# A decay recurrence as a scan on VectorE, or as a TensorE product with a triangular matrix of decay powers

## The reference

```python
DECAY = 0.95
scale = jnp.float32(np.sqrt(1.0 - DECAY))
gate = jax.nn.sigmoid(jnp.einsum('bse,em->bsm', x, Wg) + bg)
store = jnp.einsum('bse,em->bsm', x, Wv) * gate * scale
mem = smear(store, DECAY)      # mem[s] = DECAY * mem[s-1] + store[s], along the tokens
que = jax.nn.sigmoid(jnp.einsum('bse,em->bsm', x, Wq) + bq)
load = mem * que * scale
return jnp.einsum('bsm,me->bse', load, Wo)
```

```python
x = x + _L0_attn_ref(_layernorm(x, axis=-1), ...)
x = x + _L0_xattn_ref(_layernorm(x, axis=-1), ctx_512, ...)   # sim -> normalised over 256 keys -> softmax, added to x
x = x + _L0_ffn_ref(_layernorm(x, axis=-1), ...)              # argmax router, expert of each token, shared expert
```

## Time and profile before

| what | value |
| --- | --- |
| time, median of 3 executions | 166.57 us (164.66 to 167.26) |
| span of the profiled execution, first to last instruction | 155.8 us |
| TensorE busy | 119.9 us, 77% |
| VectorE busy | 108.1 us, 69% |
| GpSimd busy | 101.7 us, 65% |
| ScalarE busy | 69.8 us, 45% |

### The profile page before, as it was taken

One profiled execution on the slowest core, in us unless ns is written; L12 is line 12 of the kernel. 1 busy time (PEld: TensorE's weight loads), 2 busy tenths in 40 slices (PEclk: granted clock), 3 DMA queues, 4 the chain that ended last, 5 costly groups with the idle time before them and its releaser, 6 DMA issues. The chain is left out here.

```text
span 155.8 us, 2769 instructions
## 1 busy us (share of the span) xinstructions
PE 119.9 (77%) x709; PEld 97.2 (62%) x710; DVE 108.1 (69%) x303; ACT 69.8 (45%) x164; POOL 101.7 (65%) x145
## 2 busy tenths in 40 slices
PE   0199997997599658669879794459999979999700
PEld 0158986993387338347659594327878859888500
DVE  2672596949897999999699977122676866776510
ACT  3445878494396726794344401011434333343100
POOL 5346695696588828967858578605377776777540
PEclk9999999999999999975899999965999999999975
DMA  5997465236222251440222258283243334111000
GB/s 141 229 279 211 157 184 157 68 83 192 65 52 85 71 135 23 120 126 0 74 70 69 103 203 299 84 268 103 77 113 104 117 101 148 50 58 44 31 0 0
DMA packets 18206, 17.51 MB, mean 112 GB/s; under 512 B 4108, under 2 KB 17424, under 8 KB 18192
## 3 DMA queue, kind: packets, MB, share of 16 engines
q1 hardware_dynamic: 15792, 13.56, 30.8%
q0 software_dynamic: 1824, 3.22, 6.5%
q10 hardware_dynamic: 576, 0.56, 1.1%
HBM read 13.78 MB, written 5.38 MB: 123 GB/s over the span
## 5 line engine op out<-in xcount | busy, mean ns | idle before, releaser
L437 POOL TENSOR_TENSOR gu_lo<-stage,gu_hi 128x512 fp32r<-128x512 f32 x16 | 22.4, 1410 | 2.8 <-ACT gu_hi L502 2.8
L452 POOL DMA_INDIRECT tq<-base_rows,tid x15 | 15.4, 1026 | 13.1 <-DMA base_rows<-res 6.2
L457 POOL DMA_INDIRECT out_dram<-z,tid x15 | 15.2, 1012 | 7.6 <-DVE tid L851 2.6
L478 ACT ACTIVATE xn<-res,shift,rstd 128x256 f32<-128x256 f32 x22 | 12.0, 593 | 8.2 <-POOL shift L413 8.1
L405 POOL TENSOR_SCALAR vareps<-mv 128x2 f32<-128x2 f32 x16 | 4.2, 259 | 15.7 <-DVE mv L673 15.0
L409 POOL TENSOR_TENSOR rstd<-vareps,expo 128x2 f32<-128x2 f32 x16 | 12.4, 772 | 0.4
L1057 PE MATMUL bV<-shd,xn 128*128 128x256 f32 x32 | 9.6, 453 | 2.0 <-DVE xn L818 2.0
L670 DVE BATCH_NORM_STATS2 bn<-res 128x6 f32<-128x256 f32 x24 | 8.9, 413 | 3.0 <-DMA res<-in_x_dram 3.0
L437 POOL TENSOR_TENSOR dn_lo<-stage,dn_hi 128x512 fp32r<-128x512 f32 x8 | 11.0, 1371 | 0.0
L432 POOL DMA_INDIRECT x_sorted<-xs,dest x8 | 8.2, 1031 | 4.0 <-issue 2.6
L982 PE MATMUL bO<-wo,tq 128*128 128x256 f32 x32 | 7.8, 386 | 3.8 <-issue 2.8
(11 more groups left out here) (200 smaller groups left out, 386.4 us busy)
## 6 DMA issues: line engine op xcount, KB each, us to landing
stage<-in_L_ffn_gate_w_dram SPq DMA_DIRECT2D x8, 256.0 KB, 2.8
...
```

The costliest lines, as they stand in the source:

```text
L437: g.tensor_tensor(units[n][2], stage[:, n % RING], f32(units[n][1]), ALU.subtract).then_inc(unit_lo, 1)
L452: g.indirect_dma_start(rb[:, s % TILE_RING, :], None, base_rows, bass.IndirectOffsetOnAxis(tid[:, s:s + 1], 0), bounds_check=N - 1, oob_is ...
L457: g.indirect_dma_start(out_rows, bass.IndirectOffsetOnAxis(tid[:, s:s + 1], 0), ry[:, s % 2, :], None, bounds_check=N - 1, oob_is_err=Fals ...
L478: last = a.activation(dst[:, i, :], res[:, b * TB + i, :], ACT.Identity, bias=shift[:, kind, b, i:i + 1], scale=rstd[:, kind, b, i:i + 1])
```

## The change

The scan along the tokens becomes a product. With fade[p, t] = 0.95^(t-p) for t not under p and 0 else, mem[m, t] is the sum over s of stored[s, m] * fade[s, t]. For that the stored values must have the tokens on the partitions, so gate and value are projected token-major: for each tile of 128 tokens one product with Wg and Wv side by side, 512 columns into one PSUM bank (bG for the first tile, bV for the second). A bias along the free dimension can't be given to ScalarE, so the gate's bias is added by a further matmul of a ones matrix with two rows that hold the bias, rounded and the rest (`bg_rows`, `bg_r`, `split_bias`). `smear` multiplies in plain float32 into bank bO, the bank that `recall` writes too, and so it waits until `residual2` of the batch before has read it. `memory` falls into `store` and `load`, which are entries of their own in VectorE's list, and TensorE's list gets `gate_value` and `smear` for `gate` and `value`. The matrix `fade` is made once, by a scan of a shifted identity (`spike`).

```diff
--- before.py
+++ after.py
 PE_ORDER = """
-    turn1:0 turn_ctx:0 turn_wk:0 turn_ctx:1 kv:0 gate:0 turn1:1 value:0 query:0 kv:1 gate:1 query:1
-    turn1:2 recall:0 value:1 turn_kv:0 gate:2 query:2 value:2 turn2:0 recall:1 context_mix:0 turn1:3
-    similarity:0 recall:2 turn2:1 gate:3 context_mix:1 query:3 similarity:1 value:3 turn2:2
+    turn1:0 turn_ctx:0 turn_wk:0 turn_ctx:1 kv:0 gate_value:0 turn1:1 query:0 kv:1 smear:0 gate_value:1 query:1
+    turn1:2 recall:0 turn_kv:0 smear:1 gate_value:2 query:2 turn2:0 recall:1 context_mix:0 turn1:3
+    similarity:0 smear:2 turn2:1 gate_value:3 recall:2 context_mix:1 query:3 similarity:1 smear:3 turn2:2
     context_mix:2 turn3:0 similarity:2 recall:3 router:0 shared_up:0 router_turn:0 shared_gate:0
...
 DVE_ORDER = """
     stats1:0 weight_lo:0 norm1:0 weight_lo:1 stats1:1 weight_lo:2 turned1_lo:0 stats1:2 stats1:3
-    turned1_lo:1 memory:0 turned1_lo:2 residual2:0 memory:1 memory:2 residual2:1 turned1_lo:3
-    sim_stats:0 sim_centre:0 sim_scale:0 residual2:2 residual3:0 sim_stats:1 sim_centre:1 memory:3
+    turned1_lo:1 store:0 turned1_lo:2 load:0 store:1 residual2:0 load:1 store:2 residual2:1 turned1_lo:3
+    load:2 sim_stats:0 sim_centre:0 sim_scale:0 store:3 residual2:2 residual3:0 sim_stats:1 sim_centre:1 load:3
     sim_scale:1 sim_stats:2 turned3_lo:0 residual2:3 sim_centre:2 residual3:1 sim_scale:2
...
-        gqv_hi = sb("gqv_hi", [P, PROJ, KT, D], F32R)
-        gqv_lo = sb("gqv_lo", [P, PROJ, KT, D], F32R)
+        gv_hi = sb("gv_hi", [P, KT, 2 * D], F32R)
+        gv_lo = sb("gv_lo", [P, KT, 2 * D], F32R)
+        qw_hi = sb("qw_hi", [P, KT, D], F32R)
+        qw_lo = sb("qw_lo", [P, KT, D], F32R)
...
-        mem = sb("mem", [P, 2, W])
+        fade = sb("fade", [P, S])
+        spike = sb("spike", [P, S])
+        bg_rows = sb("bg_rows", [P, D])
+        bg_r = sb("bg_r", [P, D], F32R)
+        ones_r = sb("ones_r", [P, P], F32R)
...
+        psGV = [bG, bV]
...
-        units = [(rows(w), gqv_hi[:, i], gqv_lo[:, i]) for i, w in enumerate((Wg, Wq, Wv))]
+        units = [(rows(w), gv_hi[:, :, i * D:(i + 1) * D], gv_lo[:, :, i * D:(i + 1) * D]) for i, w in enumerate((Wg, Wv))]
+        units.append((rows(Wq), qw_hi[:, :, :], qw_lo[:, :, :]))
...
-            load("bias", hb[:, 0, :], bg.rearrange("(m p) -> p m", p=P), True)
-            load("bias", hb[:, 1, :], bq.rearrange("(m p) -> p m", p=P), True)
+            sp.wait_ge(rows_raw, 2)
+            load("bg", bg_rows[0:1, :], bg.unsqueeze(0))
+            load("bg", bg_rows[32:33, :], bg.unsqueeze(0))
+            load("bias", hb[:, :], bq.rearrange("(m p) -> p m", p=P), True)
...
+            g.memset(spike[:, :], 0.0).then_inc(ident_raw, 1)
+            g.memset(bg_rows[:, :], 0.0).then_inc(rows_raw, 1)
+            pool.wait_ge(ident_raw, 3)
+            g.affine_select(out=spike[:, :], in_=spike[:, :], compare_op=ALU.not_equal, fill=1.0, base=0,
+                            pattern=[[-1, S]], channel_multiplier=1).then_inc(spike_made, 1)
...
             def gate_tanh(b):
-                act.wait_ge(sm["g_done"], b + 1)
                 if b >= 1:
-                    act.wait_ge(sm["scanned"], b * KT)
-                for m in range(KT):
-                    last = a.activation(tg[:, m, :], psG[:, m, :], ACT.Tanh, bias=hb[:, 0, m:m + 1], scale=0.5)
-                last.then_inc(sm["tg_made"], 1)
+                    act.wait_ge(sm["mem_done"], b)
+                for i in range(TB):
+                    act.wait_ge(sm["gv_done"], b * TB + i + 1)
+                    a.activation(tg[:, i, :], psGV[i][:, 0:D], ACT.Tanh, scale=0.5).then_inc(sm["tg_made"], 1)
...
-            v.memset(ones[:, :], 1.0)
+            v.memset(ones[:, :], 1.0).then_inc(ones_made, 1)
+            dve.wait_ge(ones_made, 1)
+            v.tensor_copy(ones_r[:, :], ones[:, :]).then_inc(bg_made, 1)
...
-            def memory(b):
+            dve.wait_ge(spike_made, 1)
+            v.tensor_tensor_scan(fade[:, :], decay[:, :], spike[:, :], 0.0, ALU.mult, ALU.add).then_inc(fade_made, 1)
+
+            def split_bias():
+                dve.wait_ge(small_in["bg"], 32)
+                v.tensor_copy(bg_r[:, :], bg_rows[:, :]).then_inc(bg_made, 1)
+                dve.wait_ge(bg_made, 2)
+                v.tensor_tensor(bg_r[32:64, :], bg_rows[32:64, :], f32(bg_r[32:64, :]), ALU.subtract).then_inc(bg_made, 1)
+
+            def store(b):
+                for i in range(TB):
+                    dve.wait_ge(sm["tg_made"], b * TB + i + 1)
+                    v.scalar_tensor_tensor(tg[:, i, :], tg[:, i, :], 1.0, psGV[i][:, D:2 * D], ALU.add, ALU.mult).then_inc(sm["stored"], 1)
+
+            def load(b):
                 q = tq[:, b % 2]
-                dve.wait_ge(sm["tg_made"], b + 1)
-                dve.wait_ge(sm["v_done"], b + 1)
+                dve.wait_ge(sm["tq_made"], b + 1)
+                dve.wait_ge(sm["mem_done"], b + 1)
                 for m in range(KT):
-                    v.scalar_tensor_tensor(tg[:, m, :], tg[:, m, :], 1.0, psV[:, m, :], ALU.add, ALU.mult).then_inc(sm["stored"], 1)
-                for m in range(KT):
-                    dve.wait_ge(sm["stored"], b * KT + m + 1)
-                    v.tensor_tensor_scan(mem[:, m, 0:S], decay[:, :], tg[:, m, :], 0.0, ALU.mult, ALU.add).then_inc(sm["scanned"], 1)
-                dve.wait_ge(sm["tq_made"], b + 1)
-                for m in range(KT):
-                    dve.wait_ge(sm["scanned"], b * KT + m + 1)
-                    last = v.scalar_tensor_tensor(q[:, m, :], q[:, m, :], 1.0, mem[:, m, 0:S], ALU.add, ALU.mult)
+                    last = v.scalar_tensor_tensor(q[:, m, :], q[:, m, :], 1.0, psO[:, m, :], ALU.add, ALU.mult)
                 last.then_inc(sm["loaded"], 1)
...
-                if (name, n) == ("memory", 0):
+                if (name, n) == ("load", 0):
                     split_router()
+                if (name, n) == ("stats1", 1):
+                    split_bias()
...
-            def product(out_ap, pairs):
+            def product(out_ap, pairs, bias=None):
...
+                    if i == 0 and bias:
+                        T.matmul(*bias, start=False, stop=False)
...
+            def gate_value(b):
+                pe.wait_ge(proj_lo, 2)
+                pe.wait_ge(bg_made, 3)
+                pe.wait_ge(sm["xT1_hi_made"], b + 1)
+                pe.wait_ge(sm["xT1_lo_made"], b + 1)
+                for i in range(TB):
+                    if b >= 1:
+                        pe.wait_ge(sm["stored"], (b - 1) * TB + i + 1)
+                    rows_i = slice(i * P, (i + 1) * P)
+                    product(psGV[i][:, :], [(xT1_hi[:, b % 2, k, rows_i], xT1_lo[:, b % 2, k, rows_i], gv_hi[:, k, :], gv_lo[:, k, :])
+                                            for k in range(KT)], (psGV[i][:, 0:D], ones_r[:, :], bg_r[:, :])).then_inc(sm["gv_done"], 1)
...
+            def smear(b):
+                pe.wait_ge(fade_made, 1)
+                pe.wait_ge(sm["stored"], (b + 1) * TB)
+                if b == 0:
+                    pe.wait_ge(ctxT_made[0], 1)
+                else:
+                    pe.wait_ge(sm["x2_made"], b * TB)
+                for m in range(KT):
+                    T.matmul(psO[:, m, :], tg[:, 0, m * P:(m + 1) * P], fade[:, :], start=True, stop=False)
+                    last = T.matmul(psO[:, m, P:S], tg[:, 1, m * P:(m + 1) * P], fade[:, 0:P], start=False, stop=True)
+                last.then_inc(sm["mem_done"], 1)
```

More of the change, by code:

```diff
@@ L604, in _ @@
             for name, n in steps_of(ACT_ORDER):
-                if name in ("gate_tanh", "query_tanh") and not halved:
+                if name == "query_tanh" and not halved:
                     halve_biases()
@@ L831, in _ @@
             steps = {"stats1": stats1, "norm1": norm1, "weight_lo": weight_lo, "turned1_lo": turned1_lo,
-                     "memory": memory, "residual2": residual2, "sim_stats": sim_stats,
+                     "store": store, "load": load, "residual2": residual2, "sim_stats": sim_stats,
                      "sim_centre": sim_centre, "sim_scale": sim_scale, "residual3": residual3,
@@ L938, in project @@
                 if b >= 1:
-                    pe.wait_ge(sm[read], b * reads)
+                    pe.wait_ge(sm["tq_made"], b)
                 for m in range(KT):
-                    last = product(ps[:, m, :], [(gqv_hi[:, w, k, m * P:(m + 1) * P], gqv_lo[:, w, k, m * P:(m + 1) * P],
-                                                  xT1_hi[:, b % 2, k, :], xT1_lo[:, b % 2, k, :]) for k in range(KT)])
-                last.then_inc(sm[done], 1)
+                    last = product(psQ[:, m, :], [(qw_hi[:, k, m * P:(m + 1) * P], qw_lo[:, k, m * P:(m + 1) * P],
+                                                   xT1_hi[:, b % 2, k, :], xT1_lo[:, b % 2, k, :]) for k in range(KT)])
+                last.then_inc(sm["q_done"], 1)
+            def smear(b):
[9 more added lines that the diff above has]
+                last.then_inc(sm["mem_done"], 1)
```

(10 more changed lines are left out.)

30 lines of the change are left out of this document (15 added, 15 removed).

## The result

The changed kernel took 176.49 us, median of 4 executions (174.52 to 178.03), against 165.62 us (163.75 to 167.26) for the kernel before: 6.5% slower, ratio 1.065 with a 95% interval of 1.054 to 1.076. The forecast was 171.5 us and a loss of 3.0%; the measured time lies above its range of 166 to 175.5 us. In its profiled execution the changed kernel had a span of 174.3 us for 176.09 us of time.

What follows compares the result with a forecast made beforehand. It took a round trip of waits among TensorE, VectorE and ScalarE, in list order, as the bound. Successive delays ended at +5.1 us, taking the span from 155.8 to 160.8; with 10.8 around it, 171.5 us, range 166 to 175.5.

Steps and rivals of the forecast that it cites:

- the walk: Four-step trace of waits from turn1:2 to recall:3, then to similarity:3; claimed residual2:3 +5.1 us, span 155.8 to 160.8.
- Rival (d): Smear takes 1.8 us, not 1.4, three on the path: +1.3, 172.8 us; chance counted inside the forecast's 0.52.
- (2): From recall:0 to similarity:0 on TensorE: 12.5 us instead of 12.2, similarity:0 at 41.4, +4.5 us.
- rival (c): TensorE's clock falls at an idle gap, 26.9 or 55.8 us; some 4 us of products double: 175.5 us; chance 0.13.
- start point: Start of batch 3's similarity product, similarity:3, in the kernel before, read at 67.76 us.
- 10.8 us around the span: Time outside the profiled span, taken as 166.57 - 155.8 and added to the forecast span of 160.8.
- Rival (a): VectorE was the bound; the path loses memory:3's 3.9 us and half a microsecond of contention: 162.2 us; chance 0.15.
- the lists: Engines run written lists in order, so store:3 on VectorE can't run before the tanh; residual2:2 queues behind, +9.3 us.
- Rival (b): The delay is real, but later holes in the old path take half of +5: 168.5 us; chance 0.20.

Runs made afterwards that it cites:

- tanh_early: The changed kernel with gate_tanh:3 ahead of softmax_exp:0 on ScalarE and residual2:2 ahead of store:3 on VectorE; 175.2 us, no ratio.
- after: The changed kernel with no further edit, profiled twice; 176.49 us, ratio 1.065, and 181.97 us in the second profiled execution.
- load_first: The changed kernel with load:0 ahead of turned1_lo:2 in VectorE's list, nothing else; 176.28 us, ratio 1.041.
- filled: The changed kernel with unused matmuls in TensorE's two idle gaps, ahead of recall:0 and turn2:2; 174.92 us, ratio 1.049.
- no_scan: The kernel before with the decay scan left out, the load reading the value product in PSUM, so output differs; 161.95 us, ratio 0.967.

## Why the prediction was off

**The direction and the mechanism held.** recall:0 was forecast at 28.9 and came at 28.35; tanh_early, which changes nothing ahead of it, had it at 26.55 by its faster start, so this one agrees only to that uncertainty. From similarity:0 to residual2:2 the walk had 12.2 us (41.4 to 53.6) and the trace 12.47; store:3 queued residual2:2 behind the tanh, as it says, and undoing that in tanh_early took 3 us out of the stretch. From residual2:2 to turn2:2 it had 4.3, measured 4.74; to recall:3 another 4.0, measured 4.04; then 1.9 to residual2:3, measured 2.47. The smear was 1.3 us against 1.4, a load 0.415 against 0.41. Rival (d) is out, by the smear's 1.3 us.

**The step that failed is (2), with rival (c) beside it.** From recall:0 to similarity:0 the walk had 12.5 us; the trace had 15.39 and, with the gap filled and nothing else changed, 12.57. The walk itself put 2 us of idle TensorE ahead of recall:0 and again ahead of turn2:2, and then priced all that follows at the full clock. The fall that the earlier trace rows show behind a gap of 1.76 us was in the text as a rival with 0.13; it was the likelier case, and its price of +4 us was about right: 2.8 us in one execution, 5.0 in the other. I leaned on a gap of 1.81 us that had not done it, but the new gaps were longer (2.10 and 2.29), there were two, and one fall is enough. Behind the first of them the clock fell in all three traces that have it (after twice, tanh_early), behind the second in two of three (the second execution of after, load_first).

**The clock is the largest term of the miss, not all of it.** The time is 10.9 us over before (176.49 against 165.62), the forecast had 4.9. Without the clock, after's recall:0 (28.35) and filled's four steps put similarity:3 at 73.7; the walk has 67.76 + 5.1 = 72.9, so its steps are 0.8 us short together. And its start point was late: similarity:3 of before stands at 67.76 in that execution, at 66.56 in the second. So 5.9 us in all are missing; the clock is 2.8 to 5.0 of them, the steps 0.8 and the start point 1.2, together 4.8 to 7.0. filled's own 71.99 looks better than it is, by its faster start. Its ratio, 1.049 with the clock at 1.00 through both gaps, stays above the 1.030 of the forecast.

**The time around the span was wrong, with no effect on the sum.** The "10.8 us around the span" are 1.8 us, measured on the same execution. The other 9 were the difference between an exceptionally short execution and the median. Since the forecast was a difference added to the median, it did not suffer, but rows of that trace's later part would have misled: its 0.32 us table write is 4.34 to 4.37 in all fourteen other traces.

**Rival (a) was closer in size than in verdict.** It priced VectorE's relief at 4.4 us (166.57 to 162.2), and no_scan, which has that relief and no smear, took 6.2 us less than before, ratio 0.967. VectorE was the bound that (a) took it for. The argument against (a), the lists, is what held: the relief is real and the waits spent it. **Rival (b)**, that later holes eat the delay, fell: recall:3 to similarity:3 took 11.56 us after and 11.88 before; a shift at recall:3 goes through. Its price was also a slip: half of the 5 us leaves 169.1, not 168.5. **Not in the prediction**: sim_scale:0 at 49.76 now runs beside a weight subtraction on GpSimd, 2.85 us instead of 0.88. It lies ahead of max:0, so VectorE waited 2.22 us for the tanh and not the 4 us of the walk, and the walk's length for the stretch came out right all the same: context_mix:1 ended at 54.0 and mixed:1 could not start before that; it started at 54.37, so the collision cost at most some 0.3 us there.
